# A decoder layer on one core: row statistics moved from VectorE to ScalarE, region offsets to TensorE, and the engines' orders rewritten

## What is computed

```
x  = x + load(layernorm(x)) @ Wo     load: smear(value * sigmoid(gate)) * sigmoid(query), decay 0.95
x2 = x
x  = x2 + softmax(layernorm(sim))    sim = (layernorm(x2) @ kv) @ kv.T / 16,  kv = ctx @ W_k.T + b_k
x3 = x
x  = x3 + experts(layernorm(x3)) + shared(layernorm(x3))    8 experts, each row goes to the best one
```

## Time and profile before

| | us |
|---|---|
| median of 3 runs (lowest, highest) | 138.51 (138.19, 139.47) |
| the profiled execution | 139.09 |
| its span in the profile | 137.20 |
| busy: TensorE, VectorE, ScalarE, GpSimd | 116.0, 82.8, 75.1, 75.3 |
| first transpose of the expert loop | 86.85 |
| last matmul of the loop's chain (start) | 128.80 |

### The profile page before, as it was taken

The page is one execution under the profiler, slowest core; times in us unless marked ns, Lnnn a source line. Parts: engine busy times, 40 slices in busy tenths (PEclk is TensorE's granted clock), DMA queues, the critical chain, the costliest instruction groups (busy, mean ns, idle before and its releaser), DMA issues. The chain is left out here.

```text
span 137.2 us, 2564 instructions
## 1 busy us (share of the span) xinstructions
PE 116.0 (85%) x663; PEld 94.3 (69%) x663; DVE 82.8 (60%) x290; ACT 75.1 (55%) x193; POOL 75.3 (55%) x118
## 2 busy tenths in 40 slices
PE   0099999999999888988997997499999999999600
PEld 0059889869779574857887865378888888888300
DVE  2673099928979998739785872556454546454000
ACT  3335787695666859149573362144556465655500
POOL 5207070573856793891838799300665466456680
PEclk9999999999999999879999999999999999999975
DMA  4997992065252552104102291963426451351200
GB/s 126 249 264 207 358 302 76 0 202 185 76 160 76 193 190 76 70 16 153 62 22 81 98 313 40 301 213 81 78 56 118 72 88 42 36 63 20 30 1 0
DMA packets 18924, 16.44 MB, mean 120 GB/s; under 512 B 4320, under 2 KB 18656, under 8 KB 18912
## 3 DMA queue, kind: packets, MB, share of 16 engines
q1 hardware_dynamic: 15792, 13.56, 32.1%
q0 software_dynamic: 2544, 2.17, 9.6%
q10 hardware_dynamic: 576, 0.56, 1.2%
HBM read 11.82 MB, written 5.38 MB: 125 GB/s over the span
## 5 line engine op out<-in xcount | busy, mean ns | idle before, releaser
L480 POOL DMA_INDIRECT out_dram<-tq,tid x15 | 23.3, 1556 | 23.4 <-ACT tq L670 12.3
L466 POOL TENSOR_TENSOR gu_lo<-stage,gu_hi 128x512 fp32r<-128x512 f32 x16 | 20.3, 1286 | 2.1 <-ACT gu_hi L527 2.0
L461 POOL DMA_INDIRECT x_sorted<-xs,dest x8 | 8.6, 1074 | 5.3 <-DVE dest L821 3.1
L527 ACT CAST gu_hi<-stage 128x512 fp32r<-128x512 f32 x16 | 9.4, 618 | 0.0
L1136 PE MATMUL bV<-dn,xT 128*128 x32 | 8.3, 383 | 0.8 <-ACT xT L664 0.8
L1086 PE MATMUL bV<-shd,xn 128*128 128x256 f32 x32 | 7.9, 389 | 0.8 <-ACT xn L628 0.7
L928 PE MATMUL bT<-ident,xn 128*128 128x128 f32 x16 | 2.9, 311 | 6.6 <-DVE xn L716 6.6
L658 ACT ACTIVATE tg<-bG,meta 128x256 f32<-128x256 f32 x8 | 3.8, 474 | 7.8 <-PE bG L922 7.8
L884 DVE SCALAR_TENSOR_TENSOR tg<-tg,bG 128x256 f32<-128x256 f32 x8 | 3.4, 422 | 7.6 <-ACT tg L658 7.6
L1003 PE MATMUL bO<-wo,tq 128*128 128x256 f32 x32 | 7.9, 389 | 0.0
L703 DVE BATCH_NORM_STATS2 bn<-res 128x6 f32<-128x256 f32 x16 | 6.0, 415 | 2.5 <-DMA res<-in_x_dram 2.4
(11 more groups left out here) (204 smaller groups left out, 359.5 us busy)
## 6 DMA issues: line engine op xcount, KB each, us to landing
stage<-in_L_ffn_gate_w_dram SPq DMA_DIRECT2D x8, 256.0 KB, 3.4
stage<-in_L_ffn_up_w_dram SPq DMA_DIRECT2D x8, 256.0 KB, 3.1
dn<-in_L_ffn_down_w_dram SPq DMA_DIRECT2D x8, 256.0 KB, 3.4
xs<-x_sorted SPq DMA_DIRECT2D x15, 136.0 KB, 2.2
res<-in_x_dram SPq DMA_DIRECT2D x4, 256.0 KB, 3.8
out_dram<-res SPq DMA_DIRECT2D x4, 256.0 KB, 3.2
x_sorted<-pad SPq DMA_DIRECT2D x5, 136.0 KB, 1.8
x_sorted<-pad ACTq DMA_DIRECT2D x4, 136.0 KB, 2.5
```

Of the source, the lines that this page charges most:

```text
L461: g.indirect_dma_start(x_sorted, bass.IndirectOffsetOnAxis(dest[:, t:t + 1], 0), xs[:, t, :], None, bounds_check=E * REGION - 1, oob_is_er ...
L466: g.tensor_tensor(units[n][2], stage[:, n % RING], f32(units[n][1]), ALU.subtract).then_inc(unit_lo, 1)
L480: g.indirect_dma_start(out_rows, bass.IndirectOffsetOnAxis(tid[:, s:s + 1], 0), ry[:, s % TILE_RING, :], None, bounds_check=N - 1, oob_is_ ...
L527: a.copy(units[n][1], stage[:, n % RING]).then_inc(unit_hi, 1)
```

## The change

Five things:

- residual2 adds with tensor_tensor_reduce, which also leaves the row sum in x2_sum; MEM_SCALE moves into Wv, where weight_hi:2 and weight_lo:2 apply it. The bn_stats and bn_aggr of x2 go. POOL's centre works from x2_sum.
- ACT gets a step squares2: Square of x2 less its mean (a bias per row, and 1/D with it) with the sum along the row. sim_eps uses that.
- DVE's step sim_stats goes; ACT gets a step sim_squares: Square of sim/16, read from PSUM, with the sum. sim_rstd uses that.
- The regions' offsets enter ps_rank by one more matmul of rank (one row of ones by the row region, made once on DVE behind memory:0); destination loses its addition, and its sum is written as an integer at once.
- All four orders are new.

```diff
+    turn1:0 turn_ctx:0 turn_wk:0 turn_ctx:1 gate:0 query:0 value:0 turn1:1 kv:0 kv:1 query:1 gate:1
+    turn1:2 recall:0 value:1 turn_kv:0 gate:2 turn2:0 turn1:3 query:2 recall:1 context_mix:0 value:2
+    turn2:1 similarity:0 gate:3 query:3 recall:2 context_mix:1 value:3 similarity:1 turn2:2 turn3:0
+    context_mix:2 recall:3 similarity:2 router:0 turn2:3 shared_gu:0 context_mix:3 turn3:1
+    similarity:3 shared_turn:0 router:1 rank:0 turn3:2 rank:1 shared_gu:1 router:2 shared_gu:2
+    turn3:3 rank:2 shared_down:0 router:3 shared_turn:1 rank:3 shared_turn:2 shared_down:1
+    shared_gu:3 shared_down:2 shared_turn:3 shared_down:3
...
+    weight_hi:0 weight_hi:1 weight_hi:2 turned1_hi:0 turned_ctx:0 turned_ctx:1 turned_wk:0
+    gate_tanh:0 norm1:1 query_tanh:0 turned1_hi:1 norm1:2 kv_bias:0 weight_hi:3 norm1:3 kv_bias:1
+    turned1_hi:2 query_tanh:1 weight_hi:4 gate_tanh:1 weight_hi:5 weight_hi:6 weight_hi:7
+    weight_hi:8 weight_hi:9 turned2:0 centred:0 turned_kv:0 squares2:0 weight_hi:10 turned1_hi:3
+    gate_tanh:2 weight_hi:11 mixed:0 weight_hi:12 query_tanh:2 sim_squares:0 squares2:1 turned2:1
+    gate_tanh:3 query_tanh:3 softmax_exp:0 mixed:1 squares2:2 centred:1 sim_squares:1 turned2:2
+    squares:0 mixed:2 turned3_hi:0 weight_hi:13 softmax_exp:1 sim_squares:2 weight_hi:14 squares2:3
+    centred:2 turned2:3 score_tanh:0 shared_tanh:0 mixed:3 turned3_hi:1 softmax_exp:2 sim_squares:3
+    squares:1 squares:2 score_tanh:1 turned3_hi:2 shared_turned:0 shared_tanh:1 softmax_exp:3
+    centred:3 turned3_hi:3 score_tanh:2 shared_tanh:2 weight_hi:15 weight_hi:16 squares:3
+    weight_hi:17 shared_turned:1 weight_hi:18 score_tanh:3 shared_turned:2 shared_tanh:3
+    weight_hi:19 weight_hi:20 shared_turned:3
...
+    stats1:0 norm1:0 weight_lo:0 weight_lo:1 turned1_lo:0 weight_lo:2 stats1:1 stats1:2 stats1:3
+    turned1_lo:1 memory:0 centre_kv:0 centre_kv:1 turned1_lo:2 residual2:0 memory:1 residual2:1
+    turned1_lo:3 memory:2 sim_scale:0 residual2:2 residual3:0 memory:3 sim_scale:1 turned3_lo:0
+    residual2:3 residual3:1 route:0 sim_scale:2 shared_hidden:0 turned3_lo:1 residual3:2 route:1
+    destination:0 sim_scale:3 destination:1 turned3_lo:2 shared_hidden:1 route:2 residual3:3
+    destination:2 turned3_lo:3 shared_hidden:2 route:3 shared_add:0 destination:3 slot_table:3
+    shared_add:1 shared_hidden:3 shared_add:2 shared_add:3
...
+    rstd1:0 rstd1:1 rstd1:2 rstd1:3 weight_lo:3 weight_lo:4 centre:0 weight_lo:5 weight_lo:6
+    weight_lo:7 weight_lo:8 centre:1 weight_lo:9 sim_eps:0 sim_rstd:0 weight_lo:10 weight_lo:11
+    sim_eps:1 centre:2 sim_rstd:1 rstd3:0 sim_eps:2 centre:3 sim_rstd:2 weight_lo:12 weight_lo:13
+    sim_eps:3 weight_lo:14 row_meta:0 sim_rstd:3 rstd3:1 scatter:0 row_meta:1 rstd3:2 scatter:1
+    row_meta:2 scatter:2 rstd3:3 weight_lo:15 row_meta:3 scatter:3 weight_lo:16 weight_lo:17
+    weight_lo:18 weight_lo:19 weight_lo:20
...
+            def squares2(b):
+                act.wait_ge(sm["minus_made"], b + 1)
+                act.wait_ge(sm["x2_made"], (b + 1) * TB)
+                for i in range(TB):
...
+                    a.activation(unused2[:, :], res[:, b * TB + i, :], ACT.Square, bias=minus_m[:, b, i:i + 1],
+                                 accum_out=ssq2[:, b, i:i + 1]).then_inc(sm["squared2"], 1)
+
+            def sim_squares(b):
+                act.wait_ge(sm["sim_done"], b + 1)
+                for i in range(TB):
...
+                    a.activation(unused_s[:, :], psS[:, i, :], ACT.Square, scale=1.0 / 16.0,
+                                 accum_out=sim_ssq[:, b, i:i + 1]).then_inc(sm["sim_squared"], 1)
...
-                    v.scalar_tensor_tensor(res[:, t, :], psO[:, i, :], MEM_SCALE, res[:, t, :], ALU.mult, ALU.add).then_inc(sm["x2_made"], 1)
-                statistics(LN2, b, lambda i: res[:, b * TB + i, :], "x2_made")
-
-            def sim_stats(b):
-                dve.wait_ge(sm["sim_done"], b + 1)
-                statistics(SIM, b, lambda i: psS[:, i, :])
+                    v.tensor_tensor_reduce(res[:, t, :], psO[:, i, :], res[:, t, :], 1.0, 0.0, ALU.add, ALU.add,
+                                           x2_sum[:, b, i:i + 1]).then_inc(sm["x2_made"], 1)
...
-                v.tensor_tensor(ps_rank, ps_rank, io_reg[:, :, :], ALU.add).then_inc(sm["row_made"], 1)
-                dve.wait_ge(sm["row_made"], n)
                 v.tensor_tensor(row_e[:, :, :], ps_rank, onehot[:, tiles, :], ALU.mult).then_inc(sm["row_picked"], 1)
                 dve.wait_ge(sm["row_picked"], n)
-                v.tensor_reduce(dest_f[:, tiles], row_e[:, :, :], AX.X, ALU.add).then_inc(sm["dest_summed"], 1)
-                dve.wait_ge(sm["dest_summed"], n)
-                v.tensor_copy(dest[:, tiles], dest_f[:, tiles]).then_inc(sm["dest_made"], 1)
...
+                    v.tensor_reduce(dest[:, tiles], row_e[:, :, :], AX.X, ALU.add).then_inc(sm["dest_made"], 1)
...
-                T.matmul(ps_rank, below[:, :], onehot[:, first:first + TB, :], start=True, stop=False)
+                pe.wait_ge(rw_split, 3)
+                T.matmul(ps_rank, ones[0:1, :], region[:, :], start=True, stop=False)
+                T.matmul(ps_rank, below[:, :], onehot[:, first:first + TB, :], start=False, stop=False)
```

More of the change, by code:

```diff
@@ L34 @@
 PE_ORDER = """
[L35 to L40, removed]
@@ L186, in decoder_kernel @@
         ssq = sb("ssq", [P, B, TB])
+        ssq2 = sb("ssq2", [P, B, TB])
+        sim_ssq = sb("sim_ssq", [P, B, TB])
+        x2_sum = sb("x2_sum", [P, B, TB])
+        unused2 = sb("unused2", [P, D])
+        unused_s = sb("unused_s", [P, D])
+        region = sb("region", [1, TB * E], BF16)
         half_r2 = sb("half_r2", [P, B, TB])
@@ L193, in decoder_kernel @@
         row_e = sb("row_e", [P, TB, E])
-        dest_f = sb("dest_f", [P, NT])
         dest = sb("dest", [P, NT], U32)
@@ L526, in weight_hi @@
                 act.wait_ge(stage_in[n % RING], 16 * (n // RING + 1))
-                a.copy(units[n][1], stage[:, n % RING]).then_inc(unit_hi, 1)
+                if n == PROJ - 1:
+                    a.mul(units[n][1], stage[:, n % RING], MEM_SCALE).then_inc(unit_hi, 1)
+                else:
+                    a.copy(units[n][1], stage[:, n % RING]).then_inc(unit_hi, 1)
             def turned_wk(_):
@@ L628, in shared_turned @@
                 a.copy(hs[:, b % 2], psO).then_inc(sm["hs_made"], 1)
-            steps = {"norm1": norm1, "centred": centred, "squares": squares, "weight_hi": weight_hi, "turned_wk": turned_wk, "turned_ctx": turned_ctx, "kv_bias": kv_bias,
+            steps = {"norm1": norm1, "centred": centred, "squares": squares, "squares2": squares2, "sim_squares": sim_squares, "weight_hi": weight_hi, "turned_wk": turned_wk, "turned_ctx": turned_ctx, "kv_bias": kv_bias,
                      "turned_kv": turned_kv, "mixed": mixed, "turned1_hi": turned1_hi, "gate_tanh": gate_tanh,
@@ L721, in weight_lo @@
                 dve.wait_ge(unit_hi, n + 1)
-                v.tensor_tensor(units[n][2], stage[:, n % RING], f32(units[n][1]), ALU.subtract).then_inc(proj_lo, 1)
+                if n == PROJ - 1:
+                    v.scalar_tensor_tensor(units[n][2], stage[:, n % RING], MEM_SCALE, f32(units[n][1]), ALU.mult, ALU.subtract).then_inc(proj_lo, 1)
+                else:
+                    v.tensor_tensor(units[n][2], stage[:, n % RING], f32(units[n][1]), ALU.subtract).then_inc(proj_lo, 1)
             def turned1_lo(b):
@@ L814, in destination @@
                     v.tensor_copy(cnt[:, :], ps_count[0:1, :]).then_inc(counts_made, 1)
-                v.tensor_tensor(ps_rank, ps_rank, io_reg[:, :, :], ALU.add).then_inc(sm["row_made"], 1)
-                dve.wait_ge(sm["row_made"], n)
                 v.tensor_tensor(row_e[:, :, :], ps_rank, onehot[:, tiles, :], ALU.mult).then_inc(sm["row_picked"], 1)
                 dve.wait_ge(sm["row_picked"], n)
-                v.tensor_reduce(dest_f[:, tiles], row_e[:, :, :], AX.X, ALU.add).then_inc(sm["dest_summed"], 1)
-                dve.wait_ge(sm["dest_summed"], n)
-                v.tensor_copy(dest[:, tiles], dest_f[:, tiles]).then_inc(sm["dest_made"], 1)
+                with nc.allow_low_precision(reason="one row number and zeros are added, whole and below 2 ** 24"):
+                    v.tensor_reduce(dest[:, tiles], row_e[:, :, :], AX.X, ALU.add).then_inc(sm["dest_made"], 1)
             def slot_table(_):
```

47 lines of the change are left out of this document (19 added, 28 removed).

## The result

The changed kernel takes 141.06 us (median of 20 executions, 139.42 to 141.88) against 138.64 for the kernel before in the same comparison (20, 137.64 to 140.77): ratio 1.0139, 95% interval 1.0107 to 1.0171. It is slower by 2.4 us where 136.9 was forecast, and lies outside the range. (Ratios count undisturbed executions only, medians all of them; where a kernel's executions fall into clusters the two lie apart, so both are given.)

The account below looks back on a forecast made before the run. Bound: GpSimd's queue ahead of the expert loop, set by turn3:3's place in TensorE's order. Gains 1.03 and 1.60 less 0.86 give 1.77, less 0.2 behind: -1.57, so 136.9 us against the median 138.51; range 135.0 to 139.4.

Parts of the forecast that it names:

- The loop: From the expert loop's first transpose at 86.85 us on: nothing changes, 50.35 us of loop and tail stay.
- The clock term: turn2:3 to turn3:3: shared_gu:0, moved right behind dense work, runs at full speed, 2.82 us for 4.42; gain 1.60.
- rival 1: Thin stretch context_mix:3 to rank:1, then shared_gu:1: clock falls all the same, 1.60 given back, 138.5 us; chance 0.22.
- The order: turn2:3 to turn3:3: waits shrink from 2.03 to 1.0 us, gain 1.03; shared_gu:2 ahead of turn3:3 loses 0.86.
- The idle time ahead of turn3:2: New wait on TensorE behind router:1 and rank:0, until route:1 has read bM; taken as 1.0 us.
- the 0.86: Ahead of turn3:3, shared_gu:2 (2.82 us) stands in place of shared_down:0 and rank:2 (1.96); loss 0.86.
- the region's matmul: One more matmul in each rank on TensorE: between nothing (under others) and 0.18 us; worth nothing on the path.
- The stage up to turn2:3: TensorE's steps before turn2:3: taken as equal, between -0.5 and +1.0 us, with a possible wait at context_mix:2.
- Behind turn3:3: GpSimd from row_meta:2 on, weight_lo:15 moved ahead of row_meta:3: loss about 0.3 us, taken as 0.2.
- The Squares: 16 more activations on ACT: 0.50 us each, bounds 0.41 to 0.69, 8 us in all.
- rival 2: ACT's queue, sim_squares:1 to softmax_exp:3: Squares at 0.69 us, waiting ones block copies, 139.2 us; chance 0.14.
- Destination: Region addition and cast leave VectorE's chain, four times some 0.4 us each; worth nothing on the path.

Follow-up runs that it names:

- b2: Kernel before with 2 unused matmuls ahead of context_mix:3's wait; 138.73 us, two of its six executions below 137.
- b4: Kernel before with 2 unused matmuls ahead of context_mix:3 and 3 ahead of the expert loop; 138.69 us.
- a2: Changed kernel with 2 unused matmuls ahead of turn3:2; 138.94 us, ratio to the kernel before 0.9946.
- c1: Changed kernel with 2 unused matmuls ahead of turn3:2 and 3 ahead of the expert loop; 139.08 us, ratio 0.9988.
- h2: Changed kernel with 20 unused transposes of the identity in TensorE's idle start, ahead of turn1:0; 138.54 us, ratio 0.9973.
- Experiment 2: Kernel before with three of four matmuls of shared_down:2 and of shared_down:3 left out; 140.87 us, ratio 1.0127.
- b1: Kernel before with three of four matmuls left out in each of shared_down:2 and shared_down:3; 140.87 us, ratio 1.0127.
- a1: Changed kernel with 7 unused matmuls ahead of the expert loop; 139.45 us, ratio to the kernel before 1.0052.
- experiment 6: Changed kernel with shared_gu:2 back behind turn3:3, shared_down:0 and rank:2 ahead of it; 143.02 us, or 139.30 with 2 and 3 unused matmuls.
- c2: Kernel before with the new statistics, destination and region matmul, in the old orders; 148.57 us, ratio 1.0696.
- d1: Changed kernel with the old destination (offset added on VectorE, separate cast, no region matmul in rank); 139.86 us, ratio 1.0107.
- c3: New orders with the old statistics and old destination; 142.95 us, ratio to the kernel before 1.018.
- e2: Kernel before with the last two weight_lo (units 19 and 20) moved from GpSimd to VectorE; 138.37 us, ratio 0.9952.
- e1: Changed kernel with the last two weight_lo (units 19 and 20) moved from GpSimd to VectorE; 139.28 us, ratio 1.0016.

## Why the prediction was wrong

The profiles can be cut at turn1:1, turn2:3, turn3:3, the loop's first transpose and the end of the span. "f" marks a stretch with a fall on the path (us):

```
run      turn1:1   to turn2:3   to turn3:3   to loop   to end
before    15.59      34.64       18.43 f      18.19     50.35
b2        14.55      34.64       16.94        18.18     50.39
b4        14.22      34.65       16.90        18.27     50.26
after     15.25      35.00       18.40 f      18.34     52.81 f
a2        15.88      35.02       16.86        18.32     51.72 f
c1        14.16      34.98       18.25 f      18.33     50.38
h2        15.16      35.02       18.47 f      18.44     50.31
```

Without falls the stretches of one kernel agree from run to run within 0.13 us, and the difference of the two profiled spans, 2.60, is their sum: -0.34 (start) + 0.36 - 0.03 + 0.15 + 2.46.

*The loop: the step that failed.* "From 86.85 us on the diff touches nothing: 50.35 us of loop and tail stay." No instruction of the loop changed, and where it starts without a fall it takes 50.3 in either kernel. But the speed of its first matmuls depends on what TensorE did ahead of them. The forecast itself wrote that TensorE's own end "comes earlier too, by some 3 us, and is no longer near GpSimd's", and took that as harmless slack. It came 1.4 earlier (82.42 for 83.83, shared_down:3), GpSimd's end did not move, and the idle time brought the 2.46. Experiment 2 shows that in the old kernel too (b1: 52.72 us from the loop's first transpose to the end), and the gate_ups of a1 and c1 that it goes when the wait is filled.

*The clock term: gain 1.60, got nothing.* The step "with shared_gu:0 at 50.5 us, right behind dense work, I take full speed" is right for shared_gu:0. The fall stayed with the thin stretch of transposes and small matmuls and took shared_gu:1, the next large step behind it: rival 1, in its mechanism and size (4.36 for 2.8). It said 138.5 because it too left the loop alone.

*The order: 1.03 less 0.86 forecast, 0.06 got.* Without a fall turn2:3 to turn3:3 takes 16.86 in the new order (a2) and 16.92 in the old (b2, b4, whose fillers delay turn3:1 by 0.06). The idle time ahead of turn3:2 was right (0.93 for 1.0), and so was the 0.86 (experiment 6). What was taken as nothing on the path is the region's matmul: 0.12 and 0.11 us of TensorE in rank:0 and rank:1 (58.13 to 58.25 and 59.94 to 60.05).

*The stage up to turn2:3: 0 taken, 0.36 lost*, inside the bounds given. context_mix:2's wait for ScalarE was 0.61 where the walk had 0.7 to 0.9. That turn2:3 read 50.25 and 50.23 in the two profiles hid it: the changed run had started 0.34 sooner.

*Behind turn3:3: 0.2 taken, 0.15 found.* *The Squares* came as the rows of the neighbours said (0.51 for 0.50; from PSUM 0.38, a little below the lower bound of 0.41; with the accumulator read two in a row start 0.63 and 0.50 apart), and rival 2's mechanism, a waiting Square that blocks the copies, did not decide in the new order; in the old one it did (c2). *Destination* is worth nothing that d1 can show.

So at equal clock the change costs about 0.36 - 0.06 + 0.15 = 0.45 us. Without its clock term the forecast's own sum is -1.03 + 0.86 + 0.20 = +0.03: all of the 1.57 that it told was the clock's 1.60, and that did not come. The rest of the 2.60 between the two profiles is in the main the clock at the loop's start (2.46), less the earlier start (0.34). What stays open is why a given execution falls: a gap of 1.22 ahead of the loop was followed by a fall in c3 and not in h2, and 1.06 in b2 by none. The idle time makes a fall likelier; its length alone does not decide it here.

## What to carry to other kernels

Where an engine's clock falls in its waits, as here, its slack is not free: before calling a piece behind a wait unchanged, look at what TensorE does in the microseconds ahead of it, and count a later fall as a term of the sum. Cut two profiles at common steps before comparing them, so that a shifted start or a fall isn't taken for the edit. Keeping TensorE busy with unused work in a wait, above all ahead of the first data, can beat a finer order (137.61 for 138.61 of the kernel before; the finer order took 141.06).

## What was not expected of the hardware

- Much of the spread of executions is TensorE's clock. In the comparisons of the experiments, executions of the kernel before with a mean granted clock of 0.941 to 0.944 took 140.2 to 140.9 us, all others (0.965 to 0.989) 137.8 to 139.4. The moment at which the clock rises differs too (turn1:1 at 14.16 to 16.32 us in the profiles), and the profile's clock column does not show this: it reads 1.00 in the kernel before where pairs are 0.43 apart. In h2, where a rise and a fall come before, the same pace reads 0.53. Windows of TensorE alone, the kernel before and then h2:

```profile
10.00:12.00 2.00, 2.00 (x10) 1.00 0.82 243
```

```profile
9.00:12.00 3.00, 3.00 (x16) 0.53 0.74 235
```

- A fall needs no long idle time: in the kernel after it came at 60 us with 0.93 us in all of idle time since 50, in c1 at 57 us over TensorE's own fillers.
- Falls can stay long: 0.51 on the mean over 20 us in c2, with TensorE busy 19.15 of the 20.
- VectorE's 128x512 subtraction of 0.68 us took 1.77 where it met one of GpSimd's (e2) and 2.97 where it met two in a row (e1), and ended 0.56 us behind the last of them each time.
